# Squares and two casts of the first mixture's images move from VectorE to ScalarE, and the residual joins the attention product

## What is computed

```
x = x + L0_conv(_ln_c(x))         # y = layer norm of x; out = gamma * (y @ softmax(y^T y)) + y
t = t + L0_ffn(_ln_t(t))          # 16 experts, the two best of a token, weights of a softmax
x = x + L1_conv(_ln_c(x))         # 3x3 convolution with signs of weights
t = t + L1_ffn(_ln_t(t), edges)   # graph attention over 262144 edges gates 4 experts
```

## Time and profile before

| what | value |
|---|---|
| median of 3 runs | 1857.98 us (1856.01 to 1858.49) |
| the profiled execution's own time | 1855.4 us |
| its span in the trace | 1853.3 us |
| DVE busy | 1367.5 us (74% of the span) |
| PE busy | 912.5 us (49%) |
| ACT busy | 487.8 us (26%) |
| POOL busy | 917.8 us (50%) |

### The profile page before, as it was taken

How to read it: one execution, slowest core, us unless ns; L and a number is a source line. 1 busy time by engine, 2 the same in 40 slices (tenths; PEclk the granted TensorE clock), 3 DMA queues, 4 the chain that set the end, 5 groups by cost and what they waited for, 6 DMA issues and landing times. The chain is left out here.

```text
span 1853.3 us, 37738 instructions
## 1 busy us (share of the span) xinstructions
PE 912.5 (49%) x13313; PEld 708.8 (38%) x13313; DVE 1367.5 (74%) x2731; ACT 487.8 (26%) x974; POOL 917.8 (50%) x891
## 2 busy tenths in 40 slices
PE   1222232058889872558994445445544544445400
PEld 0222222046667652553222344434443444444300
DVE  6899998988999978983113677667766776776689
ACT  1131221144555433754442111111111111111100
POOL 0155445536666562000003777777777777777300
PEclk9855555567666655778997555555555555555555
DMA  7000000111111116012000111111111111111001
GB/s 149 5 23 23 21 18 21 39 32 41 41 43 41 40 52 105 2 47 24 0 0 6 13 13 12 13 11 13 12 13 13 12 13 12 13 12 13 7 6 40
DMA packets 113608, 46.87 MB, mean 25 GB/s; under 512 B 92503, under 2 KB 108591, under 8 KB 112802
## 3 DMA queue, kind: packets, MB, share of 16 engines
q0 software_dynamic: 27712, 20.51, 6.2%
q1 hardware_dynamic: 83666, 21.85, 6.1%
q10 hardware_dynamic: 2064, 2.10, 0.6%
HBM read 28.98 MB, written 15.89 MB: 24 GB/s over the span
## 5 line engine op out<-in xcount | busy, mean ns | idle before, releaser
L283 POOL DMA_INDIRECT edges_rows<-table,edges_src x576 | 550.6, 956 | 179.1 <-issue 175.2
L183 DVE TENSOR_TENSOR sorting_keys<-sorting_keys 128x1024 f32<-128x1024 f32 (+1 forms) x392 | 372.1, 990 | 19.8 <-ACT sorting_keys L264 18.0
L672 POOL DMA_INDIRECT y_rows<-mixture_yt,mixture_xin x143 | 181.3, 1268 | 131.0 <-ACT mixture_yt L887 84.7
L667 POOL DMA_INDIRECT x_rows<-mixture_sent,mixture_slot x128 | 158.8, 1241 | 155.9 <-DVE mixture_slot L729 117.4
L1906 ACT ACTIVATE edges_hotT<-edges_hot_ps 128x1024 bf16<-128x1024 bf16 x74 | 71.7, 1021 | 557.9 <-PE edges_hot_ps L1939 557.9
L991 PE MATMUL mixture_bank<-mixture_xT,sorting_w_part 128*128 128x128 bf16 x858 | 118.1, 259 | 48.7 <-DVE mixture_hidden L814 28.2
L1844 DVE TENSOR_TENSOR edges_raw<-edges_rows,edges_side 128x64 f32<-128x64 f32 x36 | 8.0, 221 | 175.2 <-DMA edges_rows<-table,edges_src 175.2
L991 PEld LDWEIGHTS mixture_bank<-mixture_xT,sorting_w_part 128*128 x858 | 85.5, 106 | 84.4 <-issue 75.9
L1521 DVE TENSOR_TENSOR all_eo<-publish_back,publish_ub 128x1024 f32 x16 | 19.6, 1224 | 118.7 <-PE publish_back L1548 118.7
L1728 POOL IOTA edges_part_i<- 128x64 int32 x1 | 0.2, 181 | 194.0 <-POOLq L1462 194.0
L2001 PE MATMUL edges_chain<-edges_term_parts,edges_hot 128*128 128x20 bf16 x1728 | 51.6, 179 | 90.4 <-DVE edges_term_parts L1724 90.4
(11 more groups left out here) (387 smaller groups left out, 2425.7 us busy)
## 6 DMA issues: line engine op xcount, KB each, us to landing
edges_rows<-table,edges_src POOLq DMA_INDIRECT x576, 2.4
mixture_xin<-x_rows SPq DMA_DIRECT2D x143, 49.0 KB, 1.8
all_eo<-y_rows SPq DMA_DIRECT2D x16, 256.0 KB, 4.0
y_rows<-mixture_yt,mixture_xin POOLq DMA_INDIRECT x143, 2.5
sorting_w<-in_L_ffn_w_dram SPq DMA_DIRECT2D x4, 512.0 KB, 8.9
x_rows<-mixture_sent,mixture_slot POOLq DMA_INDIRECT x128, 2.3
out_dram<-all_x_sb SPq DMA_DIRECT2D x8, 256.0 KB
constants_src_i<-in_L_ffn_edge_index_dram SPq DMA_DIRECT2D x1, 1024.0 KB, 5.0
```

The source lines that it names most:

```text
L183: self.st.mark(dve.tensor_tensor(target[half], source[0], source[1], (ALU.min, ALU.max)[half]))
L283: pool.indirect_dma_start(to, None, rows, where).then_inc(done, 16)
L667: pool.indirect_dma_start(x_rows, bass.IndirectOffsetOnAxis(ap=slot[g % 2][:, c, t:t + 1], axis=0), now[c][:, t, :], None).then_inc(scatte ...
L672: pool.indirect_dma_start(y_rows, bass.IndirectOffsetOnAxis(ap=xin[j % XB][:, ROWX - 2:ROWX - 1].bitcast(U32), axis=0), yt[j % YB][:, :], ...
```

## The change

DVE no longer squares: `center_only` stops behind the centring, ACT squares (`square`), and `variance` reduces what ACT wrote. ACT also makes the high and the middle part of `y1`, and DVE's second subtraction writes the low part as bf16 itself. `x += y` is gone: `probs` is scaled by gamma and gets the identity added, so that `y @ (gamma * m + I)` already holds `y`, and one 64 x 1 multiplication by gamma is new. The order of DVE's work is another too: `choose` now stands between the centring and the variance of n0, `locate` stands before `probs` instead of behind it, and exchanges are placed elsewhere, in the same number for each image.

```diff
--- before.py
+++ after.py
@@ -302,6 +302,8 @@
         self.rstd = a.sb(name + "_rstd", [P, groups])
         self.var_ready = a.sem(name + "_var_ready")
         self.root_ready = a.sem(name + "_root_ready")
+        self.centered = a.sem(name + "_centered")
+        self.squared = a.sem(name + "_squared")
 
     def center(self, dve, st, y, x):
         w = self.width
@@ -311,6 +313,23 @@
         st.link(dve.tensor_tensor(self.squares[:, :, :], y, y, ALU.mult))
         st.link(dve.tensor_reduce(self.var[:, :], self.squares[:, :, :], X, ALU.add))
         dve.tensor_scalar(self.var[:, :], self.var[:, :], 1.0 / w, self.eps, ALU.mult, ALU.add)\
+            .then_inc(self.var_ready, 1)
+
+    def center_only(self, dve, st, y, x, nth):
+        w = self.width
+        st.link(dve.tensor_reduce(self.mean[:, :], x, X, ALU.add))
+        st.link(dve.tensor_scalar(self.mean[:, :], self.mean[:, :], -1.0 / w, None, ALU.mult))
+        dve.tensor_tensor(y, x, per_channel(self.mean[:, :], w), ALU.add).then_inc(self.centered, 1)
+        dve.wait_ge(self.centered, nth + 1)
+
+    def square(self, act, y, nth):
+        act.wait_ge(self.centered, nth + 1)
+        act.activation(self.squares[:, :, :], y, ACT.Square).then_inc(self.squared, 1)
+
+    def variance(self, dve, st, nth):
+        dve.wait_ge(self.squared, nth + 1)
+        st.link(dve.tensor_reduce(self.var[:, :], self.squares[:, :, :], X, ALU.add))
+        dve.tensor_scalar(self.var[:, :], self.var[:, :], 1.0 / self.width, self.eps, ALU.mult, ALU.add)\
             .then_inc(self.var_ready, 1)
 
     def scale(self, dve, st, y, nth, y_ready):
@@ -584,6 +603,9 @@
         probs_ready = a.sem("probs_ready")
         mix_ready = a.sem("mix_ready")
         normed = a.sem("normed")
+        high_ready = a.sem("high_ready")
+        rest_ready = a.sem("rest_ready")
+        mid_ready = a.sem("mid_ready")
         rows_ready = a.sem("rows_ready")
         rows_turned = a.sem("rows_turned")
         xs_ready = a.sem("xs_ready")
@@ -730,39 +752,47 @@
 
             for b in range(B):
                 xb = x_sb[:, b * TB:(b + 1) * TB, :]
-                n0.vector(dve, st, y[:, :, :], xb, b, y_ready, lambda: sort.early(dve))
-                st.link(dve.tensor_tensor(xb, xb, y[:, :, :], ALU.add))
+                n0.center_only(dve, st, y[:, :, :], xb, b)
                 if b > 0:
                     choose(b - 1)
                 else:
                     sort.early(dve)
+                n0.variance(dve, st, b)
+                n0.scale(dve, st, y[:, :, :], b, y_ready)
+                sort.early(dve)
                 dve.wait_ge(gram_ready, b + 1)
                 dve.tensor_reduce(top[:, :], gram[0:C, 0:C], X, ALU.max, negate=True).then_inc(shift_ready, 1)
-                sort.early(dve)
-                dve.wait_ge(exp_ready, b + 1)
-                st.link(dve.reciprocal(part[:, :], total[:, :]))
-                dve.tensor_scalar(probs[:, :], probs[:, :], part[:, 0:1], None, ALU.mult).then_inc(probs_ready, 1)
                 if b > 0:
                     locate(b - 1)
                 else:
                     sort.early(dve)
+                dve.wait_ge(exp_ready, b + 1)
+                st.link(dve.reciprocal(part[:, :], total[:, :]))
+                st.link(dve.tensor_tensor(part[:, :], part[:, :], gam[0:C, 0:1], ALU.mult))
+                dve.scalar_tensor_tensor(probs[:, :], probs[:, :], part[:, 0:1], ident[0:C, 0:C], ALU.mult, ALU.add)\
+                    .then_inc(probs_ready, 1)
+                sort.early(dve)
                 dve.wait_ge(mix_ready, b + 1)
-                st.link(dve.scalar_tensor_tensor(xb, mix[:, :].rearrange("p (t c) -> p t c", t=TB), gam[:, 0:1],
-                                                 xb, ALU.mult, ALU.add))
-                n1.vector(dve, st, y1[:, :, :], xb, b, normed, lambda: sort.early(dve))
-                if b >= 2:
-                    dve.wait_ge(scattered[b % 2], 16 * 2 * TB * (b // 2))
+                st.link(dve.tensor_tensor(xb, mix[:, :].rearrange("p (t c) -> p t c", t=TB), xb, ALU.add))
+                n1.center_only(dve, st, y1[:, :, :], xb, b)
+                sort.early(dve)
+                n1.variance(dve, st, b)
+                sort.early(dve)
+                n1.scale(dve, st, y1[:, :, :], b, normed)
                 mid, high, low = (half_rows(sent[b % 2][0], n * C, (n + 1) * C) for n in range(3))
-                st.link(dve.tensor_copy(high, y1[:, :, :]))
-                st.link(dve.tensor_tensor(y1[:, :, :], y1[:, :, :], high, ALU.subtract))
-                st.link(dve.tensor_copy(mid, y1[:, :, :]))
-                st.link(dve.tensor_tensor(y1[:, :, :], y1[:, :, :], mid, ALU.subtract))
-                dve.tensor_copy(low, y1[:, :, :]).then_inc(rows_ready, 1)
+                sort.early(dve)
+                dve.wait_ge(normed, b + 1)
+                dve.wait_ge(high_ready, b + 1)
+                dve.tensor_tensor(y1[:, :, :], y1[:, :, :], high, ALU.subtract).then_inc(rest_ready, 1)
+                dve.wait_ge(rest_ready, b + 1)
+                dve.wait_ge(mid_ready, b + 1)
+                dve.tensor_tensor(low, y1[:, :, :], mid, ALU.subtract).then_inc(rows_ready, 1)
+                dve.wait_ge(rows_ready, b + 1)
                 if b in (2, 5):
                     weights.subtract_rough(dve, b // 3)
                 if b in (3, 6):
                     weights.subtract_middle(dve, b // 3 - 1)
-                sort.early(dve, 4)
+                sort.early(dve, 2)
             choose(B - 1)
             sort.early(dve, 2)
             locate(B - 1)
@@ -846,6 +876,7 @@
         @block.scalar
         def _(act):
             for b in range(B):
+                n0.square(act, y[:, :, :], b)
                 n0.scalar(act, b)
                 act.wait_ge(y_turned, b + 1)
                 act.activation(aT[:, :].rearrange("c (n w) -> c n w", n=2), turned[0:C, :, :], ACT.Copy).then_inc(aT_ready, 1)
@@ -855,12 +886,18 @@
                 act.wait_ge(shift_ready, b + 1)
                 act.activation(probs[:, :], gram[0:C, 0:C], ACT.Exp, bias=top[:, 0:1], accum_out=total[:, :])\
                     .then_inc(exp_ready, 1)
+                n1.square(act, y1[:, :, :], b)
                 n1.scalar(act, b)
+                act.wait_ge(normed, b + 1)
+                if b >= 2:
+                    act.wait_ge(scattered[b % 2], 16 * 2 * TB * (b // 2))
+                mid, high = (half_rows(sent[b % 2][0], n * C, (n + 1) * C) for n in range(2))
+                act.activation(high, y1[:, :, :], ACT.Copy).then_inc(high_ready, 1)
+                act.wait_ge(rest_ready, b + 1)
+                act.activation(mid, y1[:, :, :], ACT.Copy).then_inc(mid_ready, 1)
                 for n in range(2):
                     act.wait_ge(rows_turned, 2 * b + n + 1)
                     act.activation(xs[:, n, :], row_turned[n], ACT.Copy).then_inc(xs_ready, 1)
-                if b >= 2:
-                    act.wait_ge(scattered[b % 2], 16 * 2 * TB * (b // 2))
                 act.activation(half_rows(sent[b % 2][1], 0, 3 * C), half_rows(sent[b % 2][0], 0, 3 * C), ACT.Copy)\
                     .then_inc(rows_copied, 1)
                 if b in (1, 4):
```

## The result

The changed kernel is slower by a third of a percent: 1862.9 us in the median of 8 runs, beside 1857.1 us of the kernel before (also 8 runs), ratio 1.0033 with a 95% interval of 1.0023 to 1.0044 (4.3 to 8.2 us). The forecast was 1865.1. The profiled execution took 1859.5 us.

The account below looks back on a forecast made before the run. DVE was taken to bound the image loop. Images 1 to 7 at +1.54 + 1.29 - 1.57 = +1.26 us each (+8.8) and image 0 at -1.7 gave +7.1, so a median of 1865.1 us, range 1860.5 to 1869.5.

Parts of the forecast that it names:

- From the start to `y`: DVE from an image's start to the end of `y`: 7.96 us instead of 6.42, 1.54 more.
- The wait for the root: DVE idle in front of n0's reciprocal while ACT takes the root: 0.27 us, eight times.
- From `y` to the sum: DVE from the end of `y` to the sum with `mix`: 12.88 us instead of 11.59, 1.29 more.
- The wait at `locate`: DVE idle in front of `locate` until ACT's `gap_exp` ends: some 4.1 us in each of images 1 to 7.
- The three-input instruction: New instruction over 64 x 64 that ends `probs`: 0.25 us taken from a neighbour, bounds 0.17 to 0.43.
- The addition from PSUM: The sum with `mix` without its factor: 0.69 us instead of 0.75, or no gain if PSUM sets it.
- From the sum to the end: DVE from the sum with `mix` to the image's end: together 1.57 us less.
- The middle part's wait: DVE idle before the last subtraction during ACT's cast of the rest: 0.68 us with its handoffs.
- The sum: All eight images: +1.26 us in each of images 1 to 7, -1.7 in image 0, +7.1 in all.
- the squares and the logits are hidden: DVE has no idle time for ACT's squares or for the logits; other DVE work covers both.
- no wait at `locate`: Rival: `gap_exp` is out when DVE comes to `locate`, only `probs` waits; faster, 1853.7 us; chance 0.07.
- Busy time is all: Rival: DVE loses about 3.4 us an image and exchanges fill the wait for `mix`; 27 us, 1831; chance 0.01.

## Why the prediction was right

The sign, the size and the mechanism held, and the trace bears the steps out one by one, in image 2:

- **From the start to `y`**: 7.96 was predicted, and 112.54 - 104.56 = 7.98 measured. The wait for the root is 0.28, predicted as the gap of 0.27.
- **From `y` to the sum**: 12.88 predicted, 125.42 - 112.54 = 12.88 measured. The wait at `locate` is 4.08, predicted some 4.1, and ACT's `gap_exp` ends 6.45 behind `y`, as it did before. The experiments show that this chain is the cause: with `gap_exp` ahead the wait goes, with a copy more it grows.
- **The three-input instruction**, which no row showed, takes 0.28; I had 0.25 between 0.17 and 0.43. The addition from PSUM takes 0.69, as assumed.
- **From the sum to the end**: 1.57 less predicted; 145.73 - 125.42 = 20.31 beside 145.86 - 124.01 = 21.85, 1.54 less. The middle part's wait was put at 0.68 with its handoffs, 0.09 too low: ACT's cast takes 0.63, and the second subtraction starts 0.77 behind the end of the first.
- **Image 2** is 1.31 longer (1.26 predicted). The prediction took it for all of images 1 to 7; they are longer by 0.97 to 1.35, 1.22 in the mean. Image 0 takes 65.90 - 29.20 = 36.70 us, where it took 38.48: 1.8 shorter (1.7 predicted).
- **The sum**: +7.1 predicted, +6.8 in the loop, +5.8 between the medians. The forecast of 1865.1 lies 2.2 above the median, and 0.9 of that is the kernel before, which it took at 1857.98. The prediction would also have been wrong if a part behind the loop took up the delay; the spans of the two profiled executions differ by 4.4 us only, but that stretch varies by 6 us from trace to trace, and the interval (4.3 to 8.2) holds 6.8, so nothing shows that one does. That the squares and the logits are hidden held too: DVE has no idle time in front of either.

Of the rivals, *no wait at `locate`* missed its condition, as its own counter-argument said. When the condition was made true by hand, the kernel came 17 us under the one before, where that rival had 4: the load of the table left the chain of `probs` as well, and the rival had kept that exponent where it was. *Busy time is all* fell to the old order with the same contents, 6.7 us and not 27. With the same contents and an exchange at each wait the loop is 31.5 us under before, so what that rival counted is there to be had once the waits are filled.

The rule of the Trainium skill, page "ScalarE: Activation LUTs", section "Rules for kernel authors", sends additions and multiplications to VectorE. Its case here is the squares, and there the rows go the other way: 0.63 us on ACT and 0.69 on DVE for 128 x 512 in fp32, while the speed that the rule gives as its reason is for bf16. It does not name casts; that the middle cast would have stayed was my extension of it, and the cast on DVE again shows it to be right here (1.18 against 1.45 between the subtractions).

## What to carry to other kernels

Work taken off the engine that is the bound is worth what it costs there only if the result is back when the engine wants it: here 3.5 us an image were taken off, and in the old order 0.8 of them were kept. When steps are moved, count for each wait what work still stands between the instruction that feeds it and the wait; `choose` was 4.2 us of cover between `y` and the exponents that ACT takes behind it, and it was moved ahead of `y`. And look at the idle engine's queue before moving work on the busy one: one step moved on ACT was worth 22 us.

## What the runs showed of the hardware

A switch of ACT's function table costs less here than the Trainium skill has it (page "ScalarE: Activation LUTs", section "What ACT_TABLE_LOAD costs": a load of some 1283 ns and a drain of some 1380 ns, 2.66 us together). The load takes 1.28 us in every row, as stated, but in image 2 the copy before it ends at 117.47, the load begins at 117.48 and the exponent starts 0.02 behind its end: no drain shows, and the other seven images have the same gaps within 0.01.
